# Convolution groups spread over 21 steps, and the late down product at the end of its own step

## The reference

```python
x = L0_attn_u
xn = _layernorm(x, axis=-1)
k = einsum('hn,hnl->lh', W, exp(dtLam * arange(128))).real      # 128 filter taps for each channel
s = causal_convolution(k, xn) + xn * D                          # by FFT in the reference
xq = fp4_quant_dequant(xn)                                      # blocks of 16 along the last dim
h = silu(xq @ quant(w_gate).T) * (xq @ quant(w_up).T)           # 256 -> 704
g = silu(fp4_quant_dequant(h) @ quant(w_down).T)                # 704 -> 256
return x + s * g
```

## Time and profile before

| | |
|---|---|
| median of 3 runs | 602.76 us (602.55 to 604.41) |
| the profiled execution | 604.77 us |
| its span, first to last instruction | 603.0 us |
| PE busy | 480.4 us, 80% |
| DVE busy | 547.7 us, 91% |
| ACT busy | 404.6 us, 67% |
| POOL busy | 197.8 us, 33% |
| mean granted TensorE clock | 0.963 |
| moved by DMA | 70.80 MB, mean 117 GB/s |

### The profile page before, as it was taken

How to read it: one execution, slowest core, us unless ns; L and a number is a source line. 1 busy time by engine, 2 the same in 40 slices (tenths; PEclk the granted TensorE clock), 3 DMA queues, 4 the chain that set the end, 5 groups by cost and what they waited for, 6 DMA issues and landing times.

```text
span 603.0 us, 13236 instructions
## 1 busy us (share of the span) xinstructions
PE 480.4 (80%) x4956; PEld 335.4 (56%) x4956; DVE 547.7 (91%) x689; ACT 404.6 (67%) x567; POOL 197.8 (33%) x306
## 2 busy tenths in 40 slices
PE   0000366668888889999999999999999888888875
PEld 0000233236655567777777777777777655555654
DVE  6999998699999999999999999999999998989794
ACT  6962758778888876666666666666666655555562
POOL 1093000544555551111111133333332375532421
PEclk9999957789999999999999999999999989899998
DMA  5980012215222335555555555555553299440134
GB/s 172 349 258 1 1 35 88 87 25 161 88 88 89 105 89 159 157 151 151 151 156 149 157 159 158 159 158 159 158 159 89 34 158 148 81 70 1 22 50 70
DMA packets 101202, 70.80 MB, mean 117 GB/s; under 512 B 8864, under 2 KB 100768, under 8 KB 101024
## 3 DMA queue, kind: packets, MB, share of 16 engines
q1 hardware_dynamic: 93072, 61.94, 34.5%
q0 software_dynamic: 8080, 8.13, 9.4%
HBM read 61.28 MB, written 16.91 MB: 130 GB/s over the span
## 4 chain that ended last, share of the span: by engine, by line
PE 52%; DVE 31%; issue 9%; ACT 4%; POOL 2%; DMA 1%; SPq 0%; DVEq 0%; ACTq 0%; POOLq 0%
PE ps L1216 25%; PE ps L1234 9%; PE ps L1236 5%; PE ps L1225 4%; DVE work L849 4%; PE ps L1249 4%; PE ps L1253 4%; DVE wgu L936 3%; DVE work L844 3%; DVE work L875 3%; DVE work L883 2%; DVE sm L791 2%; DVE work L810 1%; PE ps L1204 1%; DVE xh L911 1%
## 5 line engine op out<-in xcount | busy, mean ns | idle before, releaser
L1216 PE MATMUL ps<-wgu,work 128*128 128x512 f16 (+1 forms) x1152 | 247.1, 370 | 10.3 <-DVE work L875 9.1
L1216 PEld LDWEIGHTS ps<-wgu,work 128*128 128x128 f16 x1152 | 113.9, 100 | 122.8 <-issue 18.9
L605 ACT ACTIVATE work<-ps,con 128x704 f32<-128x704 f32 x64 | 54.2, 848 | 121.3 <-PE ps L1216 121.3
L1234 PE MATMUL ps<-wdh,work 128*128 128x256 f16 x704 | 90.8, 279 | 2.5 <-ACT work L600 1.9
L600 ACT COPY work<-ps 128x1408 f16<-128x1408 f16 x64 | 84.9, 1327 | 10.5 <-PE ps L1225 10.5
L844 DVE SCALAR_TENSOR_TENSOR work<-work 128x960 f32<-128x960 bf16 (+2 forms) x67 | 74.1, 1123 | 14.6 <-ACT work L620 14.6
L506 POOL TENSOR_TENSOR gbuf<-gbuf,xh 128x256 f32<-128x256 f32 (+1 forms) x45 | 43.1, 1027 | 122.4 <-DVE work L857 103.5
L1225 PE MATMUL ps<-id,work 128*128 128x128 f16 x704 | 50.1, 220 | 29.7 <-DVE work L883 28.1
L1234 PEld LDWEIGHTS ps<-wdh,work 128*128 128x128 f16 x704 | 67.4, 100 | 11.1 <-ACT work L600 2.1
L849 DVE SCALAR_TENSOR_TENSOR work<-work 128x1920 f16<-128x1920 bf16 (+3 forms) x36 | 69.7, 1936 | 1.2
L810 DVE TENSOR_TENSOR work<-work,ps 128x960 f32<-128x960 f32 (+2 forms) x63 | 68.4, 1126 | 1.1
(11 more groups left out here) (152 smaller groups left out, 659.6 us busy)
## 6 DMA issues: line engine op xcount, KB each, us to landing
work<-kpad SPq DMA_DIRECT2D x64, 512.0 KB, 4.0
work<-L_attn_u SPq DMA_DIRECT2D x33, 256.0 KB, 4.5
gbuf<-u_rev SPq DMA_DIRECT2D x4, 2048.0 KB, 18.7
out<-gbuf POOLq DMA_DIRECT2D x7, 1024.0 KB, 9.3
out<-L_attn_u SPq DMA_DIRECT2D x1, 768.0 KB, 4.8
work<-L_ffn_w_down SPq DMA_DIRECT2D x1, 704.0 KB, 6.9
work<-L_ffn_w_gate SPq DMA_DIRECT2D x1, 640.0 KB, 4.7
work<-L_ffn_w_up SPq DMA_DIRECT2D x1, 640.0 KB, 5.9
```

Of the source, the lines that this page charges most:

```text
L1216: last = T.matmul(p_gu[:, a:b], xT[par][:, t, c, :], wgu[:, part, c % 2, a:b], start=(n == 0), stop=(n == len(todo) - 1))
L1234: T.matmul(dst, hT[t][:, c, :], wdh[:, c, :], start=(c == 0), stop=False)
```

## The change

The constant `S_OUT` goes. The convolution now runs in the steps 8 to 28: `groups_before` and `groups_of` give two groups to an even step and one to an odd step, 10 pairs of steps with three groups each, and the last two groups in step 28. SP's order of loads and the loops of ACT follow this. `OPEN` is worked out from the same function: the parts of the gate products open in the steps 18, 23 and 28, and the larger room begins with the last of these.

The step gets one form, with or without convolution: on PE, gate_up 1 always stands before h_transpose 1; `down` of tile 1 moves from the next step, where it stood behind the first h_transpose, to the end of its own step, behind the second group if there is one. On ACT, `silu_out` of tile 1 moves to the end of its step in the same way, `x_copy` always comes behind both squares, `y_copy` of a first group is followed by `silu_gate`, and the wait for the low parts in steps 2 to 7 asks for fewer of them.

```diff
--- before.py
+++ after.py
@@ -349,10 +349,21 @@
...
-        S_CONV, S_OUT = NP // 4, NP // 4 * 3
+        S_CONV = NP // 4
+        PAIRS = (H // G8) // 3
+        S_TAIL = S_CONV + 2 * PAIRS
+
+        def groups_before(it):
+
+            return min((it - S_CONV) // 2 * 3 + (it - S_CONV) % 2 * 2, H // G8) if it > S_CONV else 0
+
+        def groups_of(it):
+
+            return groups_before(it + 1) - groups_before(it)
+
         PEEL = 4
         FIRST = NT // 4 - 1
-        OPEN = [S_CONV + (S_OUT - S_CONV) * q1 // NQ for q0, q1 in PARTS]
+        OPEN = [min(it for it in range(NP) if groups_before(it + 1) >= q1 * C2 // G8) for q0, q1 in PARTS]
...
@@ -426,18 +437,17 @@
...
             load_t(1, 1)
-            with sp.Fori(0, (S_OUT - S_CONV) // 2 - 1) as q:
+            with sp.Fori(0, PAIRS - 1) as q:
                 for par in range(2):
                     load_x(q * 2 + (S_CONV + par + 3), 1 - par)
-                    for k in range(4):
-                        load_t(q * 8 + (4 * par + k + 2), k % 2)
-            for it in (S_OUT - 2, S_OUT - 1):
+                    for k in range(4 - 2 * par):
+                        load_t(q * 6 + (4 * par + k + 2), k % 2)
+            for it in range(S_TAIL - 2, NP - 3):
                 load_x(it + 3, (it + 1) % 2)
-                for n in range(4 * (it - S_CONV) + 2, min(4 * (it - S_CONV) + 6, H // 4)):
+                for n in range(2 * groups_before(it) + 2, min(2 * groups_before(it + 1) + 2, H // 4)):
                     load_t(n, n % 2)
-
-            for it in range(S_OUT, NP - 3):
-                load_x(it + 3, (it + 3) % 2)
+            for n in range(2 * groups_before(NP - 3) + 2, H // 4):
+                load_t(n, n % 2)
             for n in range(2):
...
@@ -532,7 +542,7 @@
...
                 ready = [(n, part) for n, part in todo if 4 * n + 3 <= it * 2 - 5 and it >= OPEN[part]]
-                for n, part in sorted(ready, key=(lambda job: (job[1], job[0])) if it < S_OUT else None):
+                for n, part in sorted(ready, key=(lambda job: (job[1], job[0])) if it < OPEN[2] else None):
                     room -= 2 if part == 0 else 1
...
@@ -554,10 +564,10 @@
...
                     a_low(it * 2 + 1)
-                if it == S_OUT:
+                if it == OPEN[2]:
                     pool.wait_ge(o_in, 16 * SEQS)
                 if it >= OPEN[0]:
-                    some_gated(it, 4 if it < S_OUT else 8)
+                    some_gated(it, 4 if it < OPEN[2] else 8)
             some_gated(NP, NP)
...
@@ -632,46 +642,40 @@
...
-            def step(it, par, x, xt, xn, gu, ch, td, a2=False, cv=False, td1=True, first=True):
+            def step(it, par, x, xt, xn, gu, ch, td, a2=False, cv=0, c0=None, first=True):
...
                     h_copy(it * 2 - 4, 0)
-                    if td1:
-                        if a2:
-                            after(act, a_lp, it * 2 - 4)
-                        silu_out(it * 2 - 5, 1, 1 - par)
                 if a2:
...
                 square(it, 1 - par, x, ch, 0)
-                if cv and xt:
-                    x_copy(it + 1, 1 - par)
                 if ch:
                     square(it, 1 - par, x, ch, 1)
-                if xt and not cv:
+                if xt:
                     x_copy(it + 1, 1 - par)
...
                     if a2:
-                        act.wait_ge(a_lp, it * 2 - 2)
+                        act.wait_ge(a_lp, it)
                     silu_out(it * 2 - 4, 0, par)
                 if cv:
-                    y_copy(it * 2 - 2 * S_CONV)
-                if td and cv:
-                    h_copy(it * 2 - 3, 1)
+                    y_copy(c0)
                 if gu:
                     silu_gate(it * 2 + 1)
-                if td and not cv:
+                if td:
                     h_copy(it * 2 - 3, 1)
...
                     down_scale(it - 1, 1 - par)
-                if cv:
-                    y_copy(it * 2 - 2 * S_CONV + 1)
+                if cv == 2:
+                    y_copy(c0 + 1)
+                if td:
+                    silu_out(it * 2 - 3, 1, par)
...
@@ -740,23 +744,19 @@
...
             for it in range(PEEL):
-                step(it, it % 2, True, it >= 1, True, True, it >= 1, it >= 2, a2=True, td1=it >= 3, first=it >= 1)
+                step(it, it % 2, True, it >= 1, True, True, it >= 1, it >= 2, a2=True, first=it >= 1)
             with act.Fori(0, (S_CONV - PEEL) // 2) as q:
...
             act.wait_ge(con_ok, 1)
-            with act.Fori(0, (S_OUT - S_CONV) // 2) as q:
+            with act.Fori(0, PAIRS) as q:
                 for par in range(2):
-                    step(q * 2 + (S_CONV + par), par, True, True, True, True, True, True, cv=True)
-            with act.Fori(0, (NP - 4 - S_OUT) // 2) as q:
-                for par in range(2):
-                    step(q * 2 + (S_OUT + par), par, True, True, True, True, True, True)
-            step(NP - 4, 0, True, True, True, True, True, True)
-            step(NP - 3, 1, True, True, False, True, True, True)
+                    step(q * 2 + (S_CONV + par), par, True, True, True, True, True, True, cv=2 - par, c0=q * 3 + 2 * par)
+            for it in range(S_TAIL, NP - 2):
+                step(it, it % 2, True, True, it < NP - 3, True, True, True, cv=groups_of(it), c0=groups_before(it))
             step(NP - 2, 0, False, True, False, True, True, True)
...
             step(NP, 0, False, False, False, False, True, True)
-            silu_out(NT - 3, 1, 0)
             for t in range(2):
...
@@ -1253,32 +1253,30 @@
...
-            def step(it, par, x, gu, td, cv=False):
+            def step(it, par, x, gu, td, cv=0):
                 if td:
...
                     h_transpose(it * 2 - 4, 0, par, copied=min(it + 1, NP))
-                    if it > 2:
-                        down(it * 2 - 5, 1)
                 if gu:
...
                     pe.wait_ge(a_lp, NT // 4)
-                    conv(it * 2 - 2 * S_CONV, 0)
+                    conv(groups_before(it), 0)
                 if td:
...
                 if cv:
-                    conv(it * 2 - 2 * S_CONV, 1)
-                if gu and not cv:
+                    conv(groups_before(it), 1)
+                if gu:
                     gate_up(it * 2 + 1, 1, par, None)
...
                     h_transpose(it * 2 - 3, 1, par, copied=it + 2 if x else None)
-                if gu and cv:
-                    gate_up(it * 2 + 1, 1, par, None)
-                if cv:
-                    conv(it * 2 - 2 * S_CONV + 1, 0)
-                    conv(it * 2 - 2 * S_CONV + 1, 1)
+                if cv == 2:
+                    conv(groups_before(it) + 1, 0)
+                    conv(groups_before(it) + 1, 1)
+                if td:
+                    down(it * 2 - 3, 1)
...
@@ -1300,11 +1298,10 @@
...
             for it in range(1, NP - 1):
-                step(it, it % 2, True, True, it >= 2, S_CONV <= it < S_OUT)
+                step(it, it % 2, True, True, it >= 2, groups_of(it) if it >= S_CONV else 0)
             step(NP - 1, 1, False, True, True)
...
-            down(NT - 3, 1)
             for t in range(2):
...
```

## The result

The changed kernel takes 613.32 us in the median of 4 runs (612.15 to 613.95) against 602.65 for the kernel before (601.08 to 604.41): a ratio of 1.0153, 95% interval 1.0126 to 1.0181, 10.7 us more. The forecast was 613.0 within 606 to 619. The execution that was profiled took 612.15, with a span of 610.3.

The account below looks back on a forecast made before the run. PE bounds convolution steps (15.36 us), DVE the others (14.37). Profiled 604.77 + 7.2 for the 21 steps + 3.0 at the end = 615.0, or 613.0 against the medians; range 606 to 619.

Parts of the forecast that it names:

- The loop of 15.70: Steps 8 to 29: one-group and two-group steps both take 15.70 us, making the 21 steps 7.2 longer.
- The ACT path: From the second tile's transposes to the down product: ACT's silu and copy take 2.37 us, which PE cannot fill.
- the wait of about 0.3: Sign in even, two-group steps: PE waits about 0.3 us before the down product, released by ACT's copy.
- The late products at the end: Last DVE chain: POOL's six products of step 31 run into it and make the end 3.0 us longer.
- the 4.4: Last DVE chain: total delay of DVE instructions by POOL's late products, where before it was 1.10 and 0.3.
- Late tables in steps 29 to 31: POOL's late tables: a wait of 1.1 us hides in PE's loop, so 0; 1 to 2 without that cover.
- Steps 2 to 7: Steps without convolution: PE's loop of 14.28 us stays under DVE's 14.37, so the new order changes nothing.
- The balance (591): First rival, convolution steps: down need not wait for the copy, the stretch takes 308, the kernel 591 us; chance 0.08.
- The clock: Third rival, PE in one-group steps: waits lower the clock, ten pairs each pay 1.66, giving 629.6 us; chance 0.06.
- filter load was late: Fourth rival, waits priced at nothing: late filter loads, or late tables with clock falls, give 617 to 620; chance 0.09.

Follow-up runs that it names:

- e1: Changed kernel, but in the convolution steps the second tile's h transposes and copy go before the second gate-up and its silu; 596.53 us, ratio 0.9863 to the kernel before.
- e4: Changed kernel, but in the convolution steps ACT takes the second tile's h copy before the silu; 611.77 us, ratio 1.0111 to the kernel before.
- e5: Changed kernel without the six gate products of step 31, so part of the output is not computed; 609.62 us.
- e7b: e7a with the store planned for step 31 held back to the last store; 594.92 us, ratio 0.9879 to the kernel before.
- e2: Changed kernel's spread groups, loads and plan, with the step order of the kernel before on PE and ACT; 607.56 us, ratio 1.0051 to the kernel before.
- e7a: e1 with the same transposes-first order also in steps 29 to 31; 596.49 us, ratio 0.9893 to the kernel before.

## Why the forecast held, point by point

**The loop of 15.70** (right, 0.04 too long). Every one of the 21 steps but one is 15.66. The ACT path is 2.33 and not 2.37: I had let the product begin 0.10 after the copy, as PE did there with the next tile's transposes, and here it begins 0.06 after it. The 21 steps were 6.6 longer, forecast 7.2. In the two-group steps the wait of about 0.3 that I had given as a sign has no row of its own: by the starts it is 259.06 less 256.73 less the 0.61 and 1.42 of work, so 0.30, and the modelled ends of the matmuls fill part of it. e1 and e4 show that this path is the cause: taken out, one-group steps fall by 1.57; shortened by 0.13, all steps fall by 0.12.

**The late products at the end** (right in size, wrong in place). Forecast 3.0, measured 3.1, and e5 shows that none of it is there without them. But I had put 2.65 of the 4.4 on L844, L849 and L883, and 2.6 of the 3.1 are on one small instruction, L834, that takes 0.25 otherwise (by lines, against the chain of before: L834 +2.62, L844 +0.52, L838 +0.42, L780 +0.15, L810 -0.32, L826 -0.29, in sum 3.1). First L834 in the kernel before, then the last chain of the changed kernel, DVE and POOL (compare rows 8):

```profile
587.08 0.25 DVE L834 TENSOR_SCALAR sm<-sm 128x176 bf16<-128x176 f32 x1
```
```profile
587.21 2.47 DVE L810 TENSOR_TENSOR work<-work,sm 128x704 f32<-128x704 f32 x2
...
590.54 0.25 DVE L826 TENSOR_TENSOR sm<-sm 128x88 f32<-128x88 f32 x1
590.58 1.60 POOL L520 DMA_DIRECT2D out<-gbuf  x1 [0.30 <-POOL gbuf L516]
590.82 2.87 DVE L834 TENSOR_SCALAR sm<-sm 128x176 bf16<-128x176 f32 x1
...
591.60 3.46 POOL L516 TENSOR_TENSOR gbuf<-gbuf,xh 128x512 f32<-128x512 f32 x3
...
593.73 0.76 DVE L838 SCALAR_TENSOR_TENSOR sm<-sm 128x176 f16<-128x176 f32 x1
594.41 1.41 DVE L844 SCALAR_TENSOR_TENSOR work<-work 128x704 f32<-128x704 bf16 x1
```

L834 comes while POOL issues its store and ends just behind the first of the three products after the store, which takes 1.91 and ends at 593.51. L810 loses less than before (2.47 against 2.79), L826 nothing. In e7b, with no store between the products, the same instruction takes 0.67:

```profile
574.38 1.09 DVE L835 TENSOR_TENSOR sm<-sm 128x88 f32<-128x88 f32 x1
575.50 0.67 DVE L843 TENSOR_SCALAR sm<-sm 128x176 bf16<-128x176 f32 x1
```

and in e5, beside a store with no product behind it, 0.25:

```profile
591.87 1.31 POOL L520 DMA_DIRECT2D out<-gbuf  x1 [0.30 <-POOL gbuf L516]
...
592.11 0.25 DVE L835 TENSOR_SCALAR sm<-sm 128x176 bf16<-128x176 f32 x1
```

So neither alone costs 2.6; a store with a product behind it does. Of the 3.1, 1.9 go when the store is held back, and 1.2 stay with the products. My walk of the queues gave the right sum by offsetting errors, and that the forecast of this term held is luck.

**Late tables in steps 29 to 31** (priced at nothing; it is 0.7). DVE waits 1.49 and 1.23 for them, and the PE loop hides it but for 0.36 to 0.5: in step 30 the first gate-up waits for DVE's product. What was right is that the loop covers most of it. In e2, with the order of before, this part is 2.5 longer than in the changed kernel (39.72 against 37.20), the fall of the clock included.

**Steps 2 to 7** (priced at nothing; they gain). From x2 to x8 all runs with the late down product at its own step's end take 85.8, the two with the old place 86.4: 0.6 less. I had the PE loop at 14.28 under DVE's 14.37; it is 14.24, and from x2 to x5 a step takes 14.24 to 14.28, so 14.37 was not DVE's limit there.

**The sum.** 6.6 + 0.7 + 3.1 - 0.6 = 9.8, against 10.2 forecast and 10.7 and 11.1 between the medians. The two terms that I had at nothing cancel, which is luck as well, and the 0.9 to 1.3 between sum and medians isn't explained; the runs of the kernel before alone lie 3.3 apart. The two executions first profiled differ by only 7.4. The difference is in the first column of the table: the part before x8 varies from 218.1 to 221.2, of which the order of the steps 2 to 7 makes 0.6. In the changed kernel step 1's gate-up ran 5.01, in the kernel before 6.64, at mixed clock levels; the changed kernel again gave 219.6. But for the 0.6 it isn't the change. A comparison of one profile with another can be off by 3 us here through this alone.

**The rivals.** The balance (591) did not come, but e1 shows that it was near: with the copy covered the 21 steps take 311.5, 11.0 less than in the kernel before and 17.5 less than in the changed one. The clock did not fall: ten waits of 1.55 left it at 1.00 in all 21 steps. Where PE stood 3.25 (e2) the lower level did come. The Trainium skill's page Perfetto Trace Analysis (Matmul Optimizations) says that the matmul engine scales its power with utilisation and asks for matmuls back to back in batches. Read as a loss by the clock, that is not borne out at waits of 1.55; the loss was the wait itself. In the changed kernel no filter load was late but for one wait of 0.3.

## What to carry to other kernels

Before spreading work to balance an engine, look at what closes each step: if a chain through another engine (here transposes, silu, copy, down product) is longer than the work put in front of its last link, work removed from the step comes back as waiting, to the hundredth. Put the longest independent block between a transpose and the product that needs its copy; the order of two blocks on two queues was worth 17 us here, more than the 11 of the balance that it was to serve. Covering one copy can uncover the next: in e7a PE stood for the copy of x in its place. And when a planner moves work later, ask what runs at the end without cover: six products moved into the last step cost 3.1 there.

## What the runs showed of the hardware that was not expected

A VectorE cast of 176 elements a partition (L834, 0.25 alone) took 2.87 when it met a GpSimd store with a product queued behind it, and 0.25 beside a store without one. Alone it does 176 elements in the 0.25 that L826 takes for 88, twice the pace. That it was held until the first product ended, at 593.5, is read from the timeline; by which lock is open. The Trainium skill's page SBUF — State Buffer (Who interferes with whom) lets a VectorE cast in its two-port modes and a GpSimd operation exclude each other for the whole of an instruction. The trace agrees in that the cast ended just behind a GpSimd product, at 593.69. It leaves open why the product went first: it began at 591.60, 0.78 after the cast.
